# A graph kernel's hops: one tile of each group gathered by PE, three by Pool, where it was two and two or one and three

## The chip, the cores and the metric

The kernel runs on one core of one Trainium2 chip. The metric is the device time of one execution in microseconds; less is better.

The engines are PE (TensorE, matmuls; its weight loads are shown as PEld), DVE (VectorE), ACT (ScalarE), Pool (GpSimd) and SP (SyncE, which here only starts transfers). Each runs its own list of instructions in order and waits on semaphores that the others raise.

## The reference

A graph of 6250 nodes with 64 features and 200,000 edges, sorted by target node `dst` (in the reference's words the head), goes through two layers. The first is a relational attention of two hops, and it is the one that the change touches:

```python
def agg(emb):
    a_input = jnp.concatenate([emb[head], emb[tail]], axis=-1)
    h = a_input @ fc_w.T + fc_b
    e = jnp.sum(h * rel_e, axis=-1)            # rel_e = relation_emb[edge_type], 50 types
    e = jnp.where(e > 0, e, LEAKY_SLOPE * e)
    m = jax.ops.segment_max(e, head, num_segments=N)
    ex = jnp.exp(e - m[head])
    w = ex / jax.ops.segment_sum(ex, head, num_segments=N)[head]
    return jax.ops.segment_sum(emb[tail] * w[:, None], head, num_segments=N) + emb
...
for _ in range(2):
    emb = agg(emb)
    emb = emb / jnp.maximum(jnp.sqrt(jnp.sum(emb * emb, axis=-1, keepdims=True)), 1e-12)
```

Here `head` is `src` and `tail` is `dst`, by the order in which the edge index is stacked. Then come a residual and a layer norm, a graph convolution whose weights a GRU cell computes, and a second residual and norm.

## The kernel before

**First phase.** The edges are sorted into 50 blocks of 125 nodes by the node that receives. They are padded to tiles of 128 edges and groups of four tiles (512 edges), so that a group belongs to one block. Beside this PE streams the GRU weights. Within a block the edges are ordered by the other node, so the first tiles of a group, the low ones, often reach into only a few neighbouring blocks of the table of node rows. `tile_at` says which tile of each group is gathered near, and in which place; the lines around 766 build it.

**The two hops** (lines 1400 to 1675, the loop over `hop`) are the part that the change touches. In each hop, 408 groups go through a pipeline of nine stages. Step `i` works on group `i` in stage 0, on group `i-1` in stage 1, and so on; eight steps are written out and looped. All engines run the same order of steps:

- SP brings the words of a group four steps ahead: `lo_d` (which node of the block each edge has, broadcast) and `code_d` (the near nodes' code, broadcast), lines 1445 and 1446. After every four groups it brings the next row numbers, `stage_idx` (line 1439), once the four groups that used them have landed.
- Pool gathers the rows of the table for the tiles that PE does not take, one indirect DMA of 128 rows for a tile (line 1477). `rows` has room for eight groups, so Pool may start on a group when PE's sum of eight groups before is finished (`summed`). Where the next group's sum is already finished it goes on without a pause.
- DVE makes the near one-hot, `hot_near` (line 1660, stage 0), the one-hot of the node in the block, `hot_t` (line 1634), adds up `x_sum` (line 1618, stage 3: PE's product and the gathered row), picks the edge's type and makes the score, keeps the running maximum (line 1626) and adds the block's sum, `block_sum` (line 1668, stage 7).
- PE in one step, in this order: the weighted sum of stage 7 (`sums`, line 1543, raises `summed`), the score products of stage 2 (line 1533, `x_rdy`), the spread of stage 4 (line 1516), the turning of the probabilities of stage 6 (line 1524, `p_turned`), and the near gather of stage 1 (line 1507, `gathered`). The gather multiplies the one-hots in f32 with the blocks of the table in SBUF.
- ACT copies the turned probabilities to `prob` (line 1569; PE's next sum waits for it), takes the exponent, stores, copies the near rows to `rows` (line 1588) and computes the bound `lower` (line 1592), in this order.

How many tiles PE gathers follows from the group's place `u`:

```python
def near_tiles(u):
    return 2 - u % 2

def near_width(u):
    return (GW, GW + GW_B)[near_tiles(u) - 1]
```

So for even groups PE gathers two tiles, one over `GW` = 2 blocks and one over `GW_B` = 3, and Pool two; for odd groups PE gathers one over two blocks, and Pool three. Each block costs two f32 matmuls in the trace's count, so ten for an even group and four for an odd one. The input needs one sweep over the blocks.

**Last phase.** The graph convolution, with its own indirect gathers by Pool (line 1854), is not touched.

Of the kernel before, what the change touches and what calls it, by code (L numbers as in the profile page):

```python
# [5 lines left out]
ALU = mybir.AluOpType  # L6
# [118 lines left out]
def gnn_kernel(nc, x, src, dst, typ, relT, fc_w, fc_b, w_ih, w_hh, h_col, h_mat, b_ih, b_hh, out):  # L125
# [49 lines left out]
    GW, GW_B = 2, 3  # L175
# [16 lines left out]
    with ExitStack() as ctx:  # L192
# [51 lines left out]
        with ExitStack() as ph:  # L244
# [278 lines left out]
            def _(dve):  # L523
                link = Chain(dve, dv, dtick1)

                def block_of(to, nodes):
# [15 lines left out]
                                                   op0=ALU.mult, op1=ALU.add))  # L542
# [4 lines left out]
                                                   op0=ALU.mult, op1=ALU.add))  # L547
                link(dve.scalar_tensor_tensor(out=idx_i[:, 2, :], in0=idx_i[:, 0, :], scalar=6, in1=idx_i[:, 2, :],
                                              op0=ALU.logical_shift_left, op1=ALU.bitwise_or))
                dve.wait_ge(iota_rdy, 4)  # L550
                for to, t in ((sort_a, slice(0, BODY)), (sort_b, slice(BODY, ES))):
                    link.mark(dve.scalar_tensor_tensor(out=to[0:PS, t], in0=blk_i[:, t], scalar=13, in1=idx_i[:, 2, t],
                                                       op0=ALU.logical_shift_left, op1=ALU.bitwise_or))
# [15 lines left out]
                                                   op0=ALU.logical_shift_left, op1=ALU.bitwise_or))  # L569
# [47 lines left out]
                while m <= SORT:  # L617
                    if m > 512:
# [12 lines left out]
                                              op0=ALU.mult, op1=ALU.add))  # L631

                for to, v in ((run_n, counts), (run_left, left), (run_quads, quads), (run_base, base)):
# [9 lines left out]
                                              op0=ALU.mult, op1=ALU.add))  # L643
                link(dve.scalar_tensor_tensor(out=run_off[:, 0:DOWN], in0=run_off[:, 0:DOWN], scalar=-4.0, in1=run_n[:, 0:DOWN],
                                              op0=ALU.add, op1=ALU.add))
# [10 lines left out]
                                              op0=ALU.add, op1=ALU.mult))  # L656
                link(dve.tensor_scalar(no_quad, field, 0.0, None, ALU.is_equal))

                for c in range(len(CUTS) - 1):
# [3 lines left out]
                    for i, k in enumerate(run_order):  # L663
                        n = c * len(run_order) + i
                        dve.wait_ge(sign_rdy, n + 1)
                        if i == 0:
                            link(dve.scalar_tensor_tensor(out=to, in0=sign[:, n % 4, 0:w], scalar=4.0, in1=iota_f[:, t],
                                                          op0=ALU.mult, op1=ALU.mult))
                        dve.scalar_tensor_tensor(out=to, in0=sign[:, n % 4, 0:w], scalar=run_step[:, k:k + 1], in1=to,
                                                 op0=ALU.mult, op1=ALU.add).then_inc(sign_used, 1)  # L670
# [10 lines left out]
                for i in range(8):  # L681
                    v, q = i // 4, i % 4
# [9 lines left out]
                                              op0=ALU.is_lt, op1=ALU.mult))  # L692
# [11 lines left out]
                                              op0=ALU.mult, op1=ALU.add))  # L704
# [15 lines left out]
                for k in range(NB):  # L720
                    for w in range(3):
                        link.mark(dve.scalar_tensor_tensor(
                            out=picked_j, in0=iota_f[:, 0:QUADS], scalar=run_rest[:, k:k + 1],
                            in1=quad_words[:, :, w].bitcast(F32), op0=ALU.is_equal, op1=ALU.mult,
# [6 lines left out]
                                              in1=run_base[:, DOWN:NB], op0=ALU.mult, op1=ALU.add))  # L731
                link.mark(dve.scalar_tensor_tensor(out=one_at[:], in0=run_left[:], scalar=-1.0, in1=rest_at[:],
                                                   op0=ALU.add, op1=ALU.add))
# [27 lines left out]
                k_f, q_f, odd_f, is_a, is_b, is_r, low, tmp1 = (tile_c[:, j:j + 1] for j in range(8))  # L761
# [4 lines left out]
                link(dve.tensor_scalar(tile_k[:, 0:1], tile_k[:, 1:2], 1, None, ALU.bitwise_and))  # L766
                link(dve.tensor_copy(odd_f, tile_k[:, 0:1]))
                link.mark(dve.tensor_scalar(is_a, k_f, 0.0, None, ALU.is_equal))
                link.mark(dve.tensor_scalar(low, odd_f, -1.0, 1.0, ALU.mult, ALU.add))
                link.sync()  # L770
                link(dve.scalar_tensor_tensor(out=is_b, in0=k_f, scalar=1.0, in1=low, op0=ALU.is_equal, op1=ALU.mult))
                link(dve.tensor_tensor(is_r, is_a, is_b, ALU.add))
                link(dve.tensor_scalar(is_r, is_r, -1.0, 1.0, ALU.mult, ALU.add))
                link.mark(dve.tensor_tensor(low, is_b, is_r, ALU.subtract))
                link(dve.scalar_tensor_tensor(out=tmp1, in0=k_f, scalar=-2.0, in1=odd_f, op0=ALU.add, op1=ALU.add))
                link.mark(dve.tensor_tensor(tmp1, tmp1, is_r, ALU.mult))
                link(dve.scalar_tensor_tensor(out=k_f, in0=is_r, scalar=3.0, in1=is_a, op0=ALU.mult, op1=ALU.add))
                link(dve.tensor_scalar(is_a, is_a, -1.0, 1.0, ALU.mult, ALU.add))
                for j, v in enumerate((k_f, is_a, low, is_r, tmp1)):
                    link.mark(dve.tensor_copy(tile_w[:, j, 0:CHUNKS], v.broadcast_to([P, CHUNKS])))  # L780
                link.mark(dve.memset(tile_w[:, 0, CHUNKS:CHUNKS + 4], 1.0))
                link.mark(dve.memset(tile_w[:, 1:3, CHUNKS + 4:], 1.0))
# [25 lines left out]
                for v, j in ((tile_g[:, 0], 0), (tile_g[:, 2], 1), (tile_h[:, 0], 2), (tile_h[:, 2], 3)):  # L808
# [5 lines left out]
                                                   op0=ALU.mult, op1=ALU.add))  # L814
# [12 lines left out]
                                              op0=ALU.mult, op1=ALU.add))  # L827
                link(dve.tensor_tensor(tile_off[:], end_group[:], n_groups[:], ALU.subtract))
                link(dve.scalar_tensor_tensor(out=tile_off[:], in0=tile_off[:], scalar=float(KT), in1=n_tiles[:],
                                              op0=ALU.mult, op1=ALU.add))  # L830
# [10 lines left out]
                def listed(b0, n):  # L841
                    for b in range(n):
# [22 lines left out]
                                              scalar=-float(NODES), in1=dst_t[:], op0=ALU.mult, op1=ALU.add))  # L865
# [389 lines left out]
        for hop in range(2):  # L1255
            with ExitStack() as ph:
# [149 lines left out]

                def near_tiles(u):

                    return 2 - u % 2

                def near_width(u):

                    return (GW, GW + GW_B)[near_tiles(u) - 1]

                def per_land(u):

                    return (KT - near_tiles(u)) * 16
# [14 lines left out]
                with nc.Block() as block:  # L1432
                    @block.sync
                    def _(sp):
# [5 lines left out]
                        def head_rows(g, u):  # L1440
                            wait_tick(sp, tick, lo_in[u % 2], rows_in(g, u) - 32)
                            wait_tick(sp, tick, lower_rdy, g - 7)
                            wait_tick(sp, tick, hot_t_rdy, g - 7)
                            n = near_width(u) * P
                            sp.dma_start(lo_wide[:, u % 8], lo_d[ds(g, 1), :].broadcast_to([P, HEAD[0]])).then_inc(lo_in[u % 2], 16)
                            sp.dma_start(code_wide[:, u % 8, 0:n], code_d[ds(g, 1), 0:n].broadcast_to([P, n])
                                         ).then_inc(lo_in[u % 2], 16)
# [17 lines left out]
                    @block.gpsimd  # L1465
                    def _(pool):

                        def half(it, h):
                            g0 = it * 8 + h * 4
                            wait_tick(pool, tick, summed, g0 - 7)  # L1470
                            wait_tick(pool, tick, staged[h], it * 16 + 16)
                            for g in range(4):
                                if g:
                                    wait_tick(pool, tick, summed, g0 + g - 7)
                                for k in range(near_tiles(g), KT):
                                    j = g * KT + k
                                    pool.indirect_dma_start(  # L1477
                                        out=rows[:, h * 4 + g, k, :], out_offset=None, in_=tab_d[hop],
                                        in_offset=bass.IndirectOffsetOnAxis(ap=stage_idx[:, h, j:j + 1], axis=0)
                                    ).then_inc(landed[h * 4 + g], 16)  # L1480
                        pool_n = live(pool)
                        for h in range(2):
                            half(0, h)
                        with loop(pool, 1, pool_n) as it:
                            for h in range(2):
                                half(it, h)
# [111 lines left out]
                    def _(dve):  # L1598
# [4 lines left out]
                        link.mark(dve.memset(block_sum[:], 0.0))  # L1603

                        def body(i, u, stages, _):

                            if stages[5]:
# [46 lines left out]
                            if stages[0]:  # L1654
                                wait(dve, lo_in[u % 2], rows_in(i, u))
                                dve.sem_inc(dtick, 1)
                                with dve.bass.Fori(0, sweeps, 1, engines=(dve.engine,)) as t:
                                    dve.wait_ge(gathered, sweeps * i + (t + past))
                                    n = near_width(u)
                                    dve.tensor_scalar(hot_near[:, u % 2, 0:n].rearrange("p b e -> p (b e)"), code_wide[:, u % 8, 0:n * P],  # L1660
                                                      node_code[:, ds(t, 1)], None, ALU.is_equal).then_inc(near_rdy, 1)
# [16 lines left out]
        with ExitStack() as ph:  # L1678
# [134 lines left out]
            with nc.Block() as block:  # L1813
# [46 lines left out]
                def _(pe):  # L1860
# [8 lines left out]
                    def load(table, start, n, top):  # L1869
                        _, v = pe.bass.values_load_multi_w_load_instructions(  # L1870
                            table[0:1, ds(start, n)], engines=(pe.engine,), min_val=0, max_val=top,
                            skip_runtime_bounds_check_because="the table is held below the number of blocks")
                        return v
# [165 lines left out]
```

## Time and profile before

| | before |
|---|---|
| median of 3 runs | 7760.88 us (7728.9 to 7768.37) |
| profiled execution | 7748.06 us, its span 7746.2 us |
| mean granted PE clock | 0.739 |
| busy PE / DVE / Pool / ACT | 4691.7 / 4197.5 / 3271.4 / 2280.1 us |
| hop 1, hop 2 (first to last x_sum) | 1836.4 to 3925.2, 4050.5 to 6148.9 us |
| indirect gathers in the hops | 2040 |

The profile is that of one execution. A busy time is the sum over an engine's instructions. The idle time of a group of instructions is that of its engine just before them, with what ended it; "remote" is a release that the profile cannot put down to an instruction of this core, and "issue" is no wait that it shows. The ends of PE's instructions are modelled. PEclk is the granted clock of PE, 1.00 for 2.4 GHz and 0.50 for 1.2 GHz.

### The profile page before, as it was taken

How to read it: one execution, taken by the hardware profiler on the slowest of the kernel's cores; microseconds unless marked ns; L12 is line 12 of the kernel's file. 1: busy time of each engine (PE TensorE's matmuls, PEld its weight loads, DVE VectorE, ACT ScalarE, POOL GpSimd, SP SyncE). 2: the span in 40 equal slices, each digit the busy share in tenths (PEclk: the TensorE clock that was granted, in tenths of full speed). 3: DMA queues.
4: the chain of work that ended last, by engine and by line, in shares of the span. 5: the costliest groups of instructions: out<-in, count | busy, mean ns of one | idle time of the engine just before them, and what ended most of it. 6: DMA issues, size and time to landing. Idle time of an engine off the chain costs nothing. (4 is left out here: it accounts for less than half of the span.)

```text
span 7746.2 us, 194542 instructions
## 1 busy us (share of the span) xinstructions
PE 4691.7 (61%) x47798; PEld 3849.7 (50%) x47800; DVE 4197.5 (54%) x17518; ACT 2280.1 (29%) x5659; POOL 3271.4 (42%) x3384
## 2 busy tenths in 40 slices
PE   4210466614777777777747777777777646666664
PEld 0000011004666676766646667667666535555553
DVE  8300477945666666666656666666666633333334
ACT  4200000003444444444424444444444311111111
POOL 0677100143444444444424444444444335555553
PEclk7555688657888888888868788888888756666656
DMA  8311699913333333333323333333333212222211
GB/s 318 151 29 47 282 420 419 419 46 81 80 79 79 82 79 79 80 80 81 78 58 80 78 77 77 82 78 81 79 80 79 52 43 48 48 46 48 47 46 39
DMA packets 506838, 827.77 MB, mean 107 GB/s; under 512 B 159444, under 2 KB 411021, under 8 KB 457585
## 3 DMA queue, kind: packets, MB, share of 16 engines
q1 hardware_dynamic: 397729, 651.81, 26.5%
q0 software_dynamic: 107936, 174.35, 9.5%
q8 instruction: 57, 0.93, 0.0%
q10 hardware_dynamic: 1072, 0.31, 0.0%
q14 instruction: 44, 0.36, 0.0%
HBM read 810.55 MB, written 13.49 MB: 106 GB/s over the span
## 5 line engine op out<-in xcount | busy, mean ns | idle before, releaser
L1477 POOL DMA_INDIRECT rows<-tab_d,stage_idx x2040 | 1955.2, 958 | 2410.1 <-PE ps_g L1543 1501.9
L1543 PE MATMUL ps_g<-rows,arena 128*128 128x65 f32 x6528 | 1062.1, 316 | 1137.9 <-issue 797.2
L1543 PEld LDWEIGHTS ps_g<-rows,arena 128*128 128x128 f32 x6528 | 975.6, 229 | 1241.7 <-issue 1110.4
L1569 ACT ACTIVATE arena<-ps_p 128x512 f32<-128x512 f32 x816 | 487.2, 597 | 2290.4 <-remote 1137.4
L1854 POOL DMA_INDIRECT tab<-y_d,stage_src x768 | 725.8, 945 | 810.4 <-issue 279.2
L479 PE MATMUL ps_gate<-ring,h_sb 128*1 128x512 f32 x3072 | 564.3, 812 | 788.3 <-DMA ring<-w_ih 537.0
L1507 PE MATMUL ps_t<-tab,hot_near 128*128 x5712 | 921.7, 302 | 38.5 <-issue 34.9
L1507 PEld LDWEIGHTS ps_t<-tab,hot_near 128*128 128x128 f32 x5712 | 784.5, 208 | 63.0 <-issue 40.1
L1946 DVE TENSOR_SCALAR to_node<-wins_list,row_all 128x384 bf16<-128x384 bf16 x864 | 279.0, 336 | 918.7 <-remote 629.4
L1626 DVE CUSTOM_DVE_ANT_0 arena<-lower,ps_s,m_old 128x512 f32<-128x512 bf16 x816 | 610.3, 748 | 175.6 <-DVE x_sum L1618 112.7
L1645 DVE SCALAR_TENSOR_TENSOR picked<-iota_f,typ_e,x_sum 128x50 f32<-128x50 f32 x3264 | 686.2, 266 | 2.9 <-issue 2.8
L1660 DVE TENSOR_SCALAR hot_near<-arena,node_code 128x640 f32<-128x640 bf16 (+1 forms) x816 | 391.0, 479 | 506.1 <-issue 374.3
L1516 PE MATMUL ps_s<-ident_f,score 128*128 128x128 f32 x3264 | 614.2, 319 | 0.0
L1618 DVE TENSOR_TENSOR x_sum<-ps_x,rows 128x200 f32<-128x200 f32 x816 | 299.3, 367 | 578.8 <-remote 553.5
L420 POOL DMA_INDIRECT rec_d<-arena,row_all x438 | 445.7, 1018 | 360.6 <-DVEq L674 219.5
L1895 PE MATMUL ps_all<-arena,to_node 128*128 128x64 bf16 x7776 | 511.6, 232 | 132.5 <-issue 124.9
L1524 PE MATMUL ps_p<-ident_f,arena 128*128 128x128 f32 x3264 | 584.5, 310 | 4.2 <-issue 3.6
L479 PEld LDWEIGHTS ps_gate<-ring,h_sb 128*1 128x1 f32 x3072 | 41.8, 81 | 1097.0 <-DMA ring<-w_ih 690.0
L1592 ACT ACTIVATE lower<-arena,far_bias 128x512 bf16<-128x512 bf16 x816 | 583.4, 715 | 0.0
L1574 ACT ACTIVATE arena<-arena,m_new 128x512 f32<-128x512 f32 x816 | 581.5, 713 | 1.4 <-DVE m_diff L1639 0.7
L2008 ACT ACTIVATE arena<-ps_all 128x384 bf16<-128x384 f32 x432 | 211.7, 490 | 1244.9 <-PE ps_all L1882 684.7
L1895 PEld LDWEIGHTS ps_all<-arena,to_node 128*128 128x128 bf16 x7776 | 434.5, 119 | 212.0 <-issue 167.2
(455 smaller groups left out, 6730.5 us busy)
## 6 DMA issues: line engine op xcount, KB each, us to landing
ring<-w_ih SPq DMA_DIRECT2D x192, 1024.0 KB
ring<-w_hh SPq DMA_DIRECT2D x192, 1024.0 KB
arena<-lo_d SPq DMA_DIRECT2D x816, 128.0 KB
arena<-code_d SPq DMA_DIRECT2D x408, 160.0 KB
rows<-tab_d,stage_idx POOLq DMA_INDIRECT x2040
arena<-list_lo_d SPq DMA_DIRECT2D x216, 128.0 KB
arena<-code_d SPq DMA_DIRECT2D x408, 64.0 KB
tab<-y_d,stage_src POOLq DMA_INDIRECT x768
```

What stands on the lines that cost most here:

```text
L479: mm = pe.matmul(ps_gate[32 * j:32 * j + 1, r % 2, :], lhsT=h_sb[:, pc:pc + 1], rhs=ring[:, n % RING, j, :], start=(pc == 0), stop=(pc == ...
L1477: pool.indirect_dma_start(out=rows[:, h * 4 + g, k, :], out_offset=None, in_=tab_d[hop], in_offset=bass.IndirectOffsetOnAxis(ap=stage_idx[ ...
L1507: mm = pe.matmul(ps_t[:, k * TW:(k + 1) * TW], lhsT=hot_near[:, p, at0 + b, :], rhs=tab[:, ds(at + b, 1), 0:TW].rearrange("p a c -> p (a c)"),
L1516: mm = pe.transpose(ps_s[:, p, k * P:(k + 1) * P], score[:, p, k:k + 1].broadcast_to([P, P]), ident_f[:])
L1524: mm = pe.transpose(ps_p[:, k * P:(k + 1) * P], prob_t[:, p, k * P:(k + 1) * P], ident_f[:])
L1543: mm = pe.matmul(ps_g[:, p, 0:C + 1], lhsT=prob[:, p, k * P:(k + 1) * P], rhs=rows[:, u, k, 0:C + 1], start=(k == 0), stop=(k == KT - 1))
L1574: act.activation(prob_t[:, q, :], masked[:, q, :], ACT.Exp, bias=m_new[:, q:q + 1], scale=-1.0)
L1592: act.activation(lower[:, (u - 1) % 4, :], lo_wide[:, (u - 1) % 8, :], ACT.Abs, bias=far_bias[:], scale=BIG).then_inc(lower_rdy, 1)
L1626: link.mark(dve.tensor_tensor_reduce(masked[:, p, :], lower[:, (u - 5) % 4, :], ps_s[:, p, :], 1.0, m_old[:, p:p + 1], ALU.add, ALU.min, m ...
L1645: link.mark(dve.scalar_tensor_tensor(out=picked[:, k, :], in0=iota_f[:, 0:R], scalar=typ_e[:, ds(g * KT + k, 1)], in1=x_sum[:, k, :], op0= ...
L1854: pool.indirect_dma_start(out=rows[:, g, k].rearrange("p j c -> p (j c)"), out_offset=None, in_=y_d, in_offset=bass.IndirectOffsetOnAxis(a ...
L1895: mm = pe.matmul(ps_total[:, ds(slots[j % KT] + k, 1), :].rearrange("p a c -> p (a c)"), lhsT=to_node[:, j % 4, k * P:(k + 1) * P], rhs=go ...
```

## The change

Each group now has one tile gathered by PE, over two blocks, and three by Pool. `near_tiles` is 1 and `near_width` is `GW` for every `u`. With them the loops change: Pool's `for k in range(near_tiles(g), KT)` issues three gathers for each group, PE's `gather` has one part of two blocks (four matmuls), DVE's `hot_near` is 256 columns wide, ACT copies 115 columns, and SP brings 64 KB of code for each group. `per_land`, the count that readers of gathered rows wait for, is 48 for each group. The table `tile_at` is built so that the low tile stands in place 0 and the three others follow.

```diff
@@ -766,17 +766,17 @@
                 link.mark(dve.tensor_scalar(is_a, k_f, 0.0, None, ALU.is_equal))
-                link.mark(dve.tensor_scalar(low, odd_f, -1.0, 1.0, ALU.mult, ALU.add))
+                link.mark(dve.memset(low, 0.0))
...
-                link(dve.scalar_tensor_tensor(out=tmp1, in0=k_f, scalar=-2.0, in1=odd_f, op0=ALU.add, op1=ALU.add))
+                link(dve.tensor_scalar(tmp1, k_f, -1.0, None, ALU.add))
...
-                for j, v in enumerate((k_f, is_a, low, is_r, tmp1)):
+                for j, v in ((0, k_f), (1, is_a), (4, tmp1)):
                     link.mark(dve.tensor_copy(tile_w[:, j, 0:CHUNKS], v.broadcast_to([P, CHUNKS])))
@@ -1406,11 +1406,11 @@
 
                 def near_tiles(u):
 
-                    return 2 - u % 2
+                    return 1
 
                 def near_width(u):
 
-                    return (GW, GW + GW_B)[near_tiles(u) - 1]
+                    return GW
```

## Rows read from the trace of the kernel before

**Rows 1.** Groups of instructions by line and shape: count | busy us, mean ns | idle us before, releasers.

```profile
L1477 POOL DMA_INDIRECT rows<-tab_d,stage_idx x2040 | 1955.2, 958 | 2410.1 <-PE ps_g L1543 1501.9 <-issue 482.1 <-remote 278.3
...
L1507 PE MATMUL ps_t<-tab,hot_near 128*128 x5712 | 921.7, 302 | 38.5 <-issue 34.9 <-DVE hot_near L1660 0.9
...
L1660 DVE TENSOR_SCALAR hot_near<-arena,node_code 128x640 f32<-128x640 bf16 x408 | 245.4, 601 | 271.6 <-issue 186.6 <-DMA arena<-code_d 44.6 <-PE ps_t L1507 36.6
...
L1660 DVE TENSOR_SCALAR hot_near<-arena,node_code 128x256 f32<-128x256 bf16 x408 | 145.6, 357 | 234.4 <-issue 187.7 <-DMA arena<-code_d 39.9 <-remote 5.7
```

**Rows 2.** Line 1618 in hop 1, then hop 2: duration ns, first and last start us.

```profile
L1618 DVE TENSOR_TENSOR x_sum<-ps_x,rows x408: 358/367/368, 1836.4 to 3925.2; 128x200 f32<-128x200 f32 x136
...
L1618 DVE TENSOR_TENSOR x_sum<-ps_x,rows x408: 358/367/368, 4050.5 to 6148.9; 128x200 f32<-128x200 f32 x136
```

**Rows 3.** Table of waits over both hops: us in total, times, longest us.

```profile
ACT arena L1569 <- remote: 1137.4, 195, 8.1
...
DVE x_sum L1618 <- remote: 553.5, 173, 18.4
```

**Rows 4.** Timeline of Pool in one round of four: start us, us, operation, idle before.

```profile
3441.97 0.94 POOL L1477 DMA_INDIRECT rows<-tab_d,stage_idx  x1 [4.68 <-PE ps_g L1543]
3443.21 0.94 POOL L1477 DMA_INDIRECT rows<-tab_d,stage_idx  x1 [0.31 <-issue]
3446.11 1.16 POOL L1477 DMA_INDIRECT rows<-tab_d,stage_idx  x1 [1.96 <-PE ps_g L1543]
...
3448.83 0.97 POOL L1477 DMA_INDIRECT rows<-tab_d,stage_idx  x1 [0.30 <-issue]
3451.33 0.94 POOL L1477 DMA_INDIRECT rows<-tab_d,stage_idx  x1 [1.52 <-remote]
...
3453.84 0.94 POOL L1477 DMA_INDIRECT rows<-tab_d,stage_idx  x1 [0.30 <-issue]
...
3456.34 0.94 POOL L1477 DMA_INDIRECT rows<-tab_d,stage_idx  x1 [0.30 <-issue]
3462.39 0.94 POOL L1477 DMA_INDIRECT rows<-tab_d,stage_idx  x1 [5.12 <-PE ps_g L1543]
```

**Rows 5.** Timeline of PE in the same round, instructions of a kind merged.

```profile
3439.14 1.94 PE L1543 MATMUL ps_g<-rows,arena 128*128 128x65 f32 x8 [3.83 <-issue]
...
3443.13 1.35 PE L1507 MATMUL ps_t<-tab,hot_near 128*128 x10
3444.31 1.01 PE L1543 MATMUL ps_g<-rows,arena 128*128 128x65 f32 x8
...
3446.41 0.68 PE L1507 MATMUL ps_t<-tab,hot_near 128*128 x4
3447.27 1.08 PE L1543 MATMUL ps_g<-rows,arena 128*128 128x65 f32 x8 [0.19 <-issue]
...
3451.60 1.08 PE L1543 MATMUL ps_g<-rows,arena 128*128 128x65 f32 x8 [0.57 <-issue]
3452.51 0.47 PE L1533 MATMUL ps_x<-a_split,hot_t 128*128 x12
...
3459.50 1.94 PE L1543 MATMUL ps_g<-rows,arena 128*128 128x65 f32 x8 [5.07 <-issue]
```

**Rows 6.** Timelines of ACT, then DVE, in the same round.

```profile
3444.97 0.36 ACT L1588 ACTIVATE rows<-ps_t 128x230 f32<-128x230 f32 x1 [0.23 <-PE ps_t L1507]
...
3450.91 0.60 ACT L1569 ACTIVATE arena<-ps_p 128x512 f32<-128x512 f32 x1 [2.12 <-PE ps_p L1524]
...
3458.81 0.60 ACT L1569 ACTIVATE arena<-ps_p 128x512 f32<-128x512 f32 x1 [5.60 <-remote]
...
3450.80 0.28 DVE L1668 SCALAR_TENSOR_TENSOR block_sum<-block_sum,alpha,ps_g 128x65 f32<-128x65 f32 x1 [0.56 <-remote]
...
3458.79 0.37 DVE L1618 TENSOR_TENSOR x_sum<-ps_x,rows 128x200 f32<-128x200 f32 x1 [3.43 <-remote]
```

**Rows 7.** Busy time behind the long hold: PE, PEld, DVE, ACT, POOL, then PEclk.

```profile
3456.70:3463.50 6.80, 4.00 (x28) 3.97 (x29) 3.18 (x17) 2.21 (x6) 1.52 (x2) 0.50 0.22 64
```

## The prediction

> **What bounds the kernel now.** The page first. The change touches only the two hops, and the slices show them as two plateaus in which every engine is partly idle, the PE busiest at seven tenths. So no engine is the bound and the answer must lie in waits. The list of groups then gives the prices of the touched operations and the idle time of their engines [rows 1]: Pool is busy 1955.2 us with its 2040 indirect gathers and idle 2410.1 us before them. The first and last x_sum of each hop give its pace [rows 2]: (3925.2 - 1836.4) / 407 = 5.13 us a group in hop 1 and (6148.9 - 4050.5) / 407 = 5.16 us in hop 2, so 5.14 us for each of 816 groups.
>
> The table of waits shows where it goes [rows 3]. ACT's copy of prob waits 1137.4 us in 195 pieces, DVE's x_sum 553.5 us in 173 pieces, for something that the profile can only call remote. 173 pieces against 816 / 4 = 204 rounds of four groups: about once in four groups.
>
> So I took one such round apart. Pool's timeline [rows 4] shows not 2, 3, 2, 3 gathers with pauses, but runs of two (3441.97, 3443.21), three (3446.11 to 3448.83) and five (3451.33 to 3456.34, with 0.30 us between neighbours). PE's timeline [rows 5] shows its work of each step already finished when the readers start [rows 6]. The fourth step is the clear one: the score products L1533 end at 3452.51 + 0.47 = 3452.98, yet x_sum, which needs them and rows gathered a step or more earlier, starts at 3458.79; at 3458.81 ACT starts the prob copy, which needs other PE work of that step; and PE itself stands still for 5.07 us until 3459.50, because its next sum needs that copy. Two engines wake within 0.02 us, so it is not one late product: PE's completions as a whole became known together, 3458.79 - 3456.34 = 2.45 us after Pool's last issue of the run. The same after the run of three: PE's sum ends at 3447.27 + 1.08 = 3448.35, but block_sum, its reader, starts at 3450.80 and ACT at 3450.91, 1.97 and 2.08 us after the issue at 3448.83. After the run of two: gather ends at 3443.13 + 1.35 = 3444.48, ACT reads it at 3444.97, 1.76 us after 3443.21.
>
> What gets through tells when the hold begins. The sum that ends at 3451.60 + 1.08 = 3452.68, 1.35 us after the first issue of the run of five, was heard (Pool went on to the next group without a pause); L1533, 1.65 us after it, was not. My reading, an inference from these times: **while Pool issues indirect gathers back to back, completions of PE are not heard from 1.5 us after the first issue until about 2 us (three gathers) or 2.45 us (five) after the last.** That, not PE's work, paces the hops. The long hold also costs the clock: in the stretch behind it the granted clock is 0.50, 1.2 GHz [rows 7], and the eight matmuls of a sum take 1.94 us in place of 1.08 [rows 5].
>
> The Trainium skill (Perfetto Trace Analysis, Tensor Engine Instruction) says that the PE's end in a profile is computed, and that its semaphore update goes out once PSUM has acknowledged the writes. That leaves room for such a hold; no row here shows the acknowledgment.
>
> **The change part by part.** Before, of two groups PE gathers two tiles and one, Pool two and three. After, PE gathers one and Pool three in each.
>
> Removed from PE: of each pair of groups, six of 14 gather matmuls. The ten take 1.35 us and the four 0.68 [rows 5], so 0.67 us a pair, 408 x 0.67 = 273 us of PE work. DVE's hot_near goes from 601 to 357 ns [rows 1]: 0.24 us a pair, 100 us; it lies in the waits of rows 3 and I count it at nothing (at most 100 us if DVE were the bound). ACT's copy is half as wide and the code rows are 64 KB for each group; both lie beside waits, nothing. The table built in the first phase has two small copies and one operation less: nothing.
>
> Added: one gather more a pair, 408 in all, each 0.94 busy and 0.30 idle, 1.25 us from issue to issue [rows 4]: 510 us of Pool. Pool has 2410 us of idle, so as work it is covered. What it does to the holds is not. SP's staging of indices waits for three landings where it waited for two in every other group, and the head rows stand behind it on SP's queue; they are asked for four groups ahead, over 20 us, so nothing unless Pool falls a whole half behind.
>
> **The new round.** I follow the same rules from a long hold on; t = 0 is a sum heard while the clock is still low (3441.08). Now every group has three gathers.
>
> - Step A. Pool's first issue comes 0.9 us after the sum (3441.97 - 3441.08), the third at 0.9 + 2.5 = 3.4. PE would end its next sum at 3445.32 - 3441.08 - 0.67 = 3.6 us, but from 0.9 + 1.5 = 2.4 us on nothing is heard, until 3.4 + 1.95 = 5.35. Here the run of two let the sum through at 4.2. A costs 5.35; PE's saving vanishes in the hold.
> - Step B. The finished results come through at once. Before, the next sum ended 3452.68 - 3450.7 = 2.0 us after that, just before the next hold begins (Pool starts 0.65 us after, plus 1.5). If it does so again, B costs 2.1 us. But the gather's result is now held too, and with it ACT's copy of it and its lower bound, which stand ahead of the next prob copy on ACT; that can cost up to 0.5 us, and then B is held as A is: 5.2 us more, then 2.1.
> - Step C. Pool now has two groups back to back, six gathers where it had five: first issue 0.75 us after, last at 0.75 + 5 x 1.25 = 7.0. Released 2.6 later (1.76, 2.0, 2.45 us for two, three, five, so about 0.2 for each), at 9.6; the next sum is heard 3461.44 - 3458.79 = 2.65 us after release, low clock included: 12.25 us after B began. B and C together 12.25.
>
> Three steps: 5.35 + 12.25 = 17.6, 5.87 us a group. Four, with a second held step: 22.8, 5.70 us. I take 5.77, nearer to the four. Against 5.14 that is 0.63 x 816 = 514 us. The profiled execution took 7748.06 us (span 7746.2); 7748 + 514 = 8262. The median of three runs is 7760.88, 13 us above it, so I say 8270 us.
>
> **The rivals.**
> - *Mild.* Every sum falls just into the hold, so no two groups merge and no long run arises: each step 0.75 + 2.5 + 1.95 = 5.2 to 5.3 us. Then 0.06 to 0.16 x 816 = 50 to 130 us, 7810 to 7890 us. For it: only 0.15 us separates heard from held in step B. Against: 173 long waits in 204 rounds say that the sum usually gets through. Chance 0.15.
> - *Heavy.* A's sum slips through as well, so that only long rounds are left: 12.25 for two groups, 6.1 us, 8550 us and a little more. Needs a sum 1.2 us earlier than I find. Chance 0.07.
> - *Faster.* If the wait in rows 3 has nothing to do with Pool's runs, then PE's step counts, and its 0.67 us a pair come off: 7761 - 273 = 7490 us. It decides if x_sum's long wait ends at the same place with six gathers as with five. For it: PE is the busiest engine and Pool idles for 2410 us. Against: the two wakings 2.45 us after Pool's last issue. Chance 0.10.
> - *No effect.* Saving and loss cancel, or the gathers are hidden and PE's saving too: 7760. Chance 0.04.
>
> The third has a rule behind it: the Trainium skill (SBUF — State Buffer, Who interferes with whom) says that PE and ACT never wait on anyone and that DMA never contends with a compute engine. By that rule the added gathers cost nothing here and PE's saving stays. The trace of before does not agree: finished PE work is read up to 5.8 us late (3458.79 - 3452.98).
>
> **How the numbers follow.** The forecast has 0.64, with 8150 (5.6 us a group) to 8400 us (5.93) as its own range. To hold 8 in 10 the range reaches down into the mild case and a little above the forecast's: 7840 to 8470. Half a per cent, 39 us, is about what a measurement can tell from no change. Slower: 0.64 + 0.15 + 0.07 = 0.86. Within: 0.04. Faster: 0.10.
>
> **What would show each step.** Pool's timeline should have runs of three and of six, none of two or five, with the first reader of PE's work 2.6 us after the last issue of a six. L1477 should stand at x2448 and L1507 at x3264, PE's busy time lower though the hops are longer. x_sum's long waits should be about 4.5 us where they were 3.4, and come once in three or four groups. x_sum's first and last start should give 5.7 to 5.9 us a group. I am wrong if runs are only threes and steps 5.2 us (mild), if PE's results are read at once within a run (faster), or if x_sum waits for rows of its own group, which would be a landing and not a hold. The last phase, with its own gathers, should not move.

## The result and the profile after

The changed kernel takes 8257.02 us (median of 4 runs, 8253.36 to 8268.52) beside 7755.7 us for the kernel before (4 runs, 7728.9 to 7768.37): ratio 1.0654, 95% interval 1.0623 to 1.0685, so 6.5% slower. The forecast was 8270 us, slower. The profiled execution took 8253.68 us, span 8251.9. Of the executions behind the experiments below one was slow, at 11710.17 us with a granted clock of 0.411 (the kernel before, beside pool_alone_b and before_paced_b), and it stands in no ratio.

First the page's head and its 40 slices, with the count of instructions behind each engine's x.

```profile
span 8251.9 us, 187610 instructions
...
PE 4638.0 (56%) x45350; PEld 3783.4 (46%) x45352; DVE 4110.8 (50%) x17516; ACT 2222.2 (27%) x5659; POOL 3636.8 (44%) x3792
...
PE   4210566326666666666646666666666646666664
...
GB/s 324 127 27 47 385 419 420 244 50 68 67 69 69 68 69 67 66 68 69 68 55 66 69 69 68 68 68 69 70 66 68 68 31 48 48 47 47 47 48 39
```

The plateaus of the two hops are at six tenths of PE where they were at seven: more time, and fewer PE instructions in it (45350 where it was 47798).

Groups of instructions by line and shape, as [rows 1]:

```profile
L1477 POOL DMA_INDIRECT rows<-tab_d,stage_idx x2448 | 2319.5, 947 | 2559.7 <-PE ps_g L1543 1788.9 <-issue 587.2 <-DMA stage_idx<-dst_e 147.9
L1507 PE MATMUL ps_t<-tab,hot_near 128*128 x3264 | 654.5, 331 | 18.0 <-issue 17.3 <-DVE hot_near L1660 0.5
...
L1660 DVE TENSOR_SCALAR hot_near<-arena,node_code 128x256 f32<-128x256 bf16 x816 | 302.7, 371 | 488.9 <-issue 365.8 <-DMA arena<-code_d 96.5 <-remote 25.4
```

Pool has its 408 gathers more and is nevertheless idle longer before them, 2559.7 us where it was 2410.1. PE's gather matmuls fell by 921.7 - 654.5 = 267 us.

The first and last x_sum of each hop, as [rows 2]:

```profile
L1618 DVE TENSOR_TENSOR x_sum<-ps_x,rows x408: 361/367/369, 1817.1 to 4184.6; 128x200 f32<-128x200 f32 x136
...
L1618 DVE TENSOR_TENSOR x_sum<-ps_x,rows x408: 353/367/369, 4299.9 to 6655.3; 128x200 f32<-128x200 f32 x136
```

(4184.6 - 1817.1) / 407 = 5.82 us a group in hop 1 and (6655.3 - 4299.9) / 407 = 5.79 us in hop 2, where [rows 2] gave 5.13 and 5.16. That is 0.66 x 816 = 537 us in the hops. Some 29 us come back ahead of hop 1 (x_sum starts at 1817.1, not 1836.4) and between the hops (115.3 us, not 125.3). The stretch from the last x_sum to the end is 8251.9 - 6655.3 = 1596.6 us, before 1597.3.

The table of waits over both hops, as [rows 3] (us in total, times, longest):

```profile
ACT arena L1569 <- remote: 1740.3, 251, 7.6
...
DVE x_sum L1618 <- remote: 1131.0, 243, 13.9
```

x_sum waits 1131.0 / 243 = 4.65 us each time (before 553.5 / 173 = 3.2), once in 816 / 243 = 3.4 groups.

One round of the changed kernel. Pool's timeline, as [rows 4]:

```profile
3490.48 0.94 POOL L1477 DMA_INDIRECT rows<-tab_d,stage_idx  x1 [5.31 <-PE ps_g L1543]
...
3492.97 0.96 POOL L1477 DMA_INDIRECT rows<-tab_d,stage_idx  x1 [0.30 <-issue]
3495.69 0.94 POOL L1477 DMA_INDIRECT rows<-tab_d,stage_idx  x1 [1.76 <-PE ps_g L1543]
...
3502.03 0.95 POOL L1477 DMA_INDIRECT rows<-tab_d,stage_idx  x1 [0.30 <-issue]
3507.93 0.95 POOL L1477 DMA_INDIRECT rows<-tab_d,stage_idx  x1 [4.95 <-PE ps_g L1543]
```

PE's, as [rows 5]:

```profile
3492.68 1.08 PE L1543 MATMUL ps_g<-rows,arena 128*128 128x65 f32 x8 [0.19 <-issue]
...
3495.90 1.08 PE L1543 MATMUL ps_g<-rows,arena 128*128 128x65 f32 x8 [0.39 <-issue]
3496.82 0.47 PE L1533 MATMUL ps_x<-a_split,hot_t 128*128 x12
...
3505.20 1.94 PE L1543 MATMUL ps_g<-rows,arena 128*128 128x65 f32 x8 [6.46 <-issue]
```

ACT's and DVE's, as [rows 6]:

```profile
3504.50 0.60 ACT L1569 ACTIVATE arena<-ps_p 128x512 f32<-128x512 f32 x1 [7.09 <-remote]
...
3495.17 0.28 DVE L1668 SCALAR_TENSOR_TENSOR block_sum<-block_sum,alpha,ps_g 128x65 f32<-128x65 f32 x1 [0.69 <-PE ps_g L1543]
...
3504.49 0.37 DVE L1618 TENSOR_TENSOR x_sum<-ps_x,rows 128x200 f32<-128x200 f32 x1 [4.89 <-remote]
```

The reader is to see a run of three (3490.48 to 3492.97), then six (3495.69 to 3502.03). The sum that ends at 3492.68 + 1.08 = 3493.76 is read by block_sum only at 3495.17, 2.20 us after the last issue of the three. The score products end at 3496.82 + 0.47 = 3497.29 and x_sum starts at 3504.49, 7.2 us later and 2.46 us after the last issue of the six; ACT starts 0.01 us after it. The window behind it, as [rows 7]:

```profile
3504.40:3508.50 4.10, 3.30 (x25) 3.33 (x26) 3.00 (x17) 2.21 (x6) 0.57 (x1) 0.50 0.23 65
```

The granted clock is again 0.50 (1.2 GHz), and the sum takes 1.94 us in place of 1.08.

### The profile page after: what moved, and what is told of

Same layout as the page of the kernel before. It is cut to its first block and busy times, and to the rows that moved or that the text cites. A ratio compares the mean times of both kernels' runs of the same rounds, so it can differ in the third digit from the quotient of the medians.

```text
span 8251.9 us, 187610 instructions
## 1 busy us (share of the span) xinstructions
PE 4638.0 (56%) x45350; PEld 3783.4 (46%) x45352; DVE 4110.8 (50%) x17516; ACT 2222.2 (27%) x5659; POOL 3636.8 (44%) x3792
## 5 line engine op out<-in xcount | busy, mean ns | idle before, releaser
L1477 POOL DMA_INDIRECT rows<-tab_d,stage_idx x2448 | 2319.5, 947 | 2559.7 <-PE ps_g L1543 1788.9
L1543 PE MATMUL ps_g<-rows,arena 128*128 128x65 f32 x6528 | 1154.2, 334 | 1718.3 <-issue 1253.9
L1543 PEld LDWEIGHTS ps_g<-rows,arena 128*128 128x128 f32 x6528 | 1059.3, 246 | 1824.2 <-issue 1556.1
L1569 ACT ACTIVATE arena<-ps_p 128x512 f32<-128x512 f32 x816 | 487.2, 597 | 2892.9 <-remote 1740.3
L479 PE MATMUL ps_gate<-ring,h_sb 128*1 128x512 f32 x3072 | 573.1, 824 | 776.7 <-DMA ring<-w_ih 548.3
L1618 DVE TENSOR_TENSOR x_sum<-ps_x,rows 128x200 f32<-128x200 f32 x816 | 299.4, 367 | 1144.7 <-remote 1131.0
L1626 DVE CUSTOM_DVE_ANT_0 arena<-lower,ps_s,m_old 128x512 f32<-128x512 bf16 x816 | 610.2, 748 | 200.8 <-DVE x_sum L1618 111.6
L1516 PE MATMUL ps_s<-ident_f,score 128*128 128x128 f32 x3264 | 664.6, 339 | 0.1
L1507 PE MATMUL ps_t<-tab,hot_near 128*128 x3264 | 654.5, 331 | 18.0 <-issue 17.3
L1524 PE MATMUL ps_p<-ident_f,arena 128*128 128x128 f32 x3264 | 630.9, 329 | 0.8 <-ACT alpha L1576 0.7
L420 POOL DMA_INDIRECT rec_d<-arena,row_all x438 | 445.9, 1018 | 360.2 <-DVEq L674 219.5
L1574 ACT ACTIVATE arena<-arena,m_new 128x512 f32<-128x512 f32 x816 | 581.2, 712 | 0.4 <-DVE m_diff L1639 0.4
L1660 DVE TENSOR_SCALAR hot_near<-arena,node_code 128x256 f32<-128x256 bf16 x816 | 302.7, 371 | 488.9 <-issue 365.8
L1507 PEld LDWEIGHTS ps_t<-tab,hot_near 128*128 128x128 f32 x3264 | 524.8, 229 | 42.1 <-issue 18.8
L479 PEld LDWEIGHTS ps_gate<-ring,h_sb 128*1 128x1 f32 x3072 | 41.9, 81 | 1093.7 <-DMA ring<-w_ih 705.5
```

The lines of the kernel that those rows point to most:

```text
L479: mm = pe.matmul(ps_gate[32 * j:32 * j + 1, r % 2, :], lhsT=h_sb[:, pc:pc + 1], rhs=ring[:, n % RING, j, :], start=(pc == 0), stop=(pc == ...
L1477: pool.indirect_dma_start(out=rows[:, h * 4 + g, k, :], out_offset=None, in_=tab_d[hop], in_offset=bass.IndirectOffsetOnAxis(ap=stage_idx[ ...
L1507: mm = pe.matmul(ps_t[:, k * TW:(k + 1) * TW], lhsT=hot_near[:, p, at0 + b, :], rhs=tab[:, ds(at + b, 1), 0:TW].rearrange("p a c -> p (a c)"),
L1516: mm = pe.transpose(ps_s[:, p, k * P:(k + 1) * P], score[:, p, k:k + 1].broadcast_to([P, P]), ident_f[:])
L1524: mm = pe.transpose(ps_p[:, k * P:(k + 1) * P], prob_t[:, p, k * P:(k + 1) * P], ident_f[:])
L1543: mm = pe.matmul(ps_g[:, p, 0:C + 1], lhsT=prob[:, p, k * P:(k + 1) * P], rhs=rows[:, u, k, 0:C + 1], start=(k == 0), stop=(k == KT - 1))
```

## The experiments

The first eight kernels, and two of the last four, met chips on which the kernel before takes 5936 to 5942 us, not 7756. Those six chips turned out to be a control of their own; the last two kernels met a chip on which it takes 7744. No chip was met twice in the experiments, so whether the difference lies in the chip or in a state it was in is not known; "chip" below means the chip as it was met.

**Theory.** The hold that the prediction read from the trace: the length of Pool's runs of indirect gathers decides how long PE's results are not heard. **Rivals.** The gathers' own work or landing makes the loss, or PE's, ACT's and DVE's parts of the change do.

**pe_alone.** PE leaves six matmuls of each pair out, and DVE, ACT and SP do only what they do in the changed kernel; Pool stays as before. So nobody gathers the second tile of even groups: its rows stay zero, and the kernel does not compute the reference's values.

```
+def pool_from(u):
+    return 2 - u % 2
-for k in range(near_tiles(g), KT):
+for k in range(pool_from(g), KT):
```

> PE's part of the change alone: one near tile for each group on PE, DVE, ACT and SP as in the changed kernel, but Pool's gathers stay 2, 3, 2, 3; the second tile of even groups is left out (its rows are zero). Theory of the hold: Pool's runs stay two, three and five, the long hold stays, and only the step behind it, the one whose sum gets through, is shorter by up to 0.67 us in a round of four: 204 x 0.67 = 137 us, so about 7620 us. Rival (PE's work paces the hops): 273 us less, 7490 us. Rival (nothing of PE counts): 7760 us.

5890.95 us beside 5941.27: ratio 0.9914 (0.9897 to 0.993).

**pool_alone.** The opposite: PE's fourteen matmuls stay, and in even groups Pool gathers a third tile too, into a buffer that nobody reads. Whoever reads the group's rows waits for its landing too (`per_land` is 48).

```
+if near_tiles(g) == 2:
+    pool.indirect_dma_start(out=unused[:, h * 2 + g // 2, :], ...)
```

> Pool's part alone: the kernel before with its PE work, but in even groups Pool issues one gather more, into a spare tile that nobody reads, and readers of the rows wait for its landing too. Theory of the hold: runs of three and six, 5.8 us a group or a little more, 8250 to 8350 us. Rival (Pool's added issues are covered by its idle time): 7760 us. Rival (the loss comes from reading rows that PE no longer supplies): 7760 us too.

5911.79 us beside 5941.27: ratio 0.995 (0.9933 to 0.9966). The added gathers cost nothing on this chip; the kernel is even 0.5% faster.

**after_paced and before_paced.** One wait more on Pool ahead of each group's gathers, in the kernel after and in the one before: it takes them up only when PE has also turned the probabilities of the step whose sum it waits for (`p_turned`). No work is added or left out; the wait is meant to keep the gathers of two groups apart.

```
 wait_tick(pool, tick, summed, g0 - 7)
+wait_tick(pool, tick, p_turned, g0 - 6)
...
 wait_tick(pool, tick, summed, g0 + g - 7)
+wait_tick(pool, tick, p_turned, g0 + g - 6)
```

> The changed kernel with one wait more on Pool: before a group's gathers it also waits until PE has turned the probabilities of the same step. Theory of the hold: that completion is held during a run, so two groups can't merge, all runs are of three, and each step costs about 0.75 + 2.5 + 1.95 = 5.2 us: 816 x 0.6 less, about 7780 us. Rival (Pool is too slow with three gathers, or rows land too late): an added wait can only make it later, 8260 us or more.

> The kernel before with the same added wait on Pool. Theory of the hold: runs of two and three in turn, none of five; a step with a run of three costs 5.2 us, one with a run of two is let through at about 4.2 us, 4.7 us on average where it was 5.14: 0.44 x 816 = 360 us less, about 7400 us. Rival: 7760 us or more.

5889.64 us (0.991, 0.9893 to 0.9926) and 5913.86 us (0.9952, 0.9936 to 0.9969). No theory had expected any of these four times, since all counted from 7756 or 8257. Nor does the pause do here what it was meant to: the trace of before_paced still has 87 runs of five gathers in hop 1, so on this chip it says nothing on the length of the runs. Something else was different, and the next runs asked what.

**probe_hold.** A kernel by itself, with none of the case's computation: PE and ACT hand a one-column product to and fro 760 times, DVE copies one column in a chain, and Pool meanwhile issues runs of 1 to 8 indirect gathers.

```
for j in range(n):
    pool.indirect_dma_start(out=got[:, j, :], in_=pairs, in_offset=idx[:, j:j + 1], ...)
...
pe.wait_ge(taken, t); pe.matmul(ps[:, 0:1], ...).then_inc(made, 1)
act.wait_ge(made, t + 1); act.activation(took[:], ps[:, 0:1], ACT.Copy).then_inc(taken, 1)
```

> This kernel computes nothing of the reference: it copies x to the output, and beside that PE and ACT play ping-pong (one small matmul, one small copy of it, each waiting for the other), DVE runs a chain of small copies that wait for each other, and Pool issues runs of 1, 2, 3, 4, 5, 6 and 8 indirect gathers of 128 rows of 512 bytes, then runs of 3 and 6 plain transfers; then SP issues 3 and 6. Theory of the hold: in each run of n indirect gathers ACT does not hear PE from about 1.5 us after the first issue until about 2 us after the last, so the gap between two ACT copies is about 1.25 (n - 1) + 0.5 us or more, 1.8 us for two, 3.0 for three, 5.5 for five, 6.8 for six, while DVE's chain goes on without a gap. SP's transfers leave no gap. For Pool's plain transfers it says nothing. Rival (the readers in the hops wait for their own rows to land, or for Pool): no gap in any run, since nothing here waits for a landing but Pool.

The table of waits of probe_hold:

```profile
PEld ps L66 <- ACT took L72: 261.0, 759, 0.3
...
PE ps L66 <- ACT took L72: 199.5, 759, 0.3
```

Of 759 waits of PE for ACT none is over 0.3 us, with up to eight gathers back to back; each turn takes 0.446 to 0.448 us. There is no hold here. The kernel before took 5939.43 us beside it.

**after_again and before_again.** The two kernels unaltered.

> The changed kernel itself, unaltered, beside the kernel before on whichever chip this job gets. In the jobs so far the kernel before took 5941 and 5939 us, 1815 us less than in the runs shown with the result, and the ping-pong of PE and ACT went on every 0.446 us through all of Pool's gathers: no hold there. Theory of the hold: the loss of 6.5% is made by the hold alone. Where the kernel before takes about 5940 us, the changed one then gains what it takes off PE and DVE, 0 to 1.5%, 5850 to 5940 us; where it takes about 7756 us, the changed one is again at 8257 us. Rival (Pool's third gather costs by its own time or its landing): 3 to 6% slower on either chip.

> The kernel before, unaltered, as one of the runs, so that its trace can be read on a chip of this job. Theory of the hold: if it takes about 5940 us, its trace shows x_sum and ACT's prob copy without the 2 to 6 us waits behind Pool's runs, the hops at about 4.2 us a group, and in the first phase the weights streaming on through Pool's long run of scatters, where the trace shown with the prediction has 29 and 47 GB/s in two slices. Rival (chips of these jobs are quicker all over): instructions and landings themselves are shorter in the same proportion, 23%. The ratio to the kernel before, which is itself, shows what a comparison of this kind can tell.

5881.71 us beside 5940.91: ratio 0.9902 (0.9886 to 0.9919); and 5942.05 us, ratio to itself 1.0002. **The same change is 1.0% faster here and 6.5% slower there.** The chips hardly differ in how fast Pool, DVE and ACT execute: L1477 has a mean of 955 ns in before_again (958 there), DVE's L1626 748 (748), ACT's L1569 597 (597). PE's matmuls are shorter (L1543 277 ns, 316 there) at a higher granted clock (0.889, there 0.739), but PE's busy time differs by only 4691.7 - 4378.6 = 313 us of the 1810 between the spans. The rest lies in waits. Page slices, then the table of waits from 1180 to 4420 us (hop 1 and most of hop 2), of before_again:

```profile
GB/s 288 413 419 418 417 418 397 16 109 99 99 99 99 98 97 96 99 99 99 65 88 98 97 96 97 99 96 95 98 98 95 97 20 68 69 69 69 68 70 49
...
ACT arena L1569 <- PE ps_p L1524: 945.4, 726, 2.9
POOL rows L1477 <- PE ps_g L1543: 807.4, 412, 4.3
...
ACT arena L1574 <- DVE m_diff L1639: 377.8, 646, 2.8
```

ACT's copy has no wait for something remote, where [rows 3] has 195; nor has it any when the table is taken over both hops. Pool's timeline of before_again, then ACT's and DVE's beside it, with a run of five:

```profile
2023.35 0.94 POOL L1477 DMA_INDIRECT rows<-tab_d,stage_idx  x1 [3.34 <-PE ps_g L1543]
...
2028.35 0.94 POOL L1477 DMA_INDIRECT rows<-tab_d,stage_idx  x1 [0.30 <-issue]
```

```profile
2028.00 0.60 ACT L1569 ACTIVATE arena<-ps_p 128x512 f32<-128x512 f32 x1 [1.11 <-PE ps_p L1524]
...
2027.50 0.37 DVE L1618 TENSOR_TENSOR x_sum<-ps_x,rows 128x200 f32<-128x200 f32 x1
```

x_sum and ACT's copy start 4.15 and 4.65 us into the run, before its last issue; where the hold is, both came 2.45 us after it [rows 4, 6].

**wide_near.** The changed kernel with near_width left at (GW + GW_B, GW) in turn, so that DVE's and SP's part isn't narrower. This asks where the 1% comes from. ACT's copy stays half as wide, as in the changed kernel.

> The changed kernel with one part undone: in even groups SP brings 160 KB of code and DVE makes hot_near 640 columns wide again, of which PE reads only the first 256. PE, ACT and Pool stay as changed. On a chip without the hold DVE starts x_sum without waiting, so the theory there is that DVE's own time paces the hops, and that the 1% that the changed kernel gains is the narrower hot_near: 563 - 358 = 205 ns x 408 = 84 us at most, 59 measured. Then this kernel is back at the time of the kernel before, 5930 to 5945 us. Rival (PE's six matmuls for each pair make the gain): it stays at about 5882 us. If the job gets a chip where the kernel before takes about 7756 us, DVE's width lies in the holds and this kernel takes 8257 us as the changed one.

5892.5 us beside 5940.52: 0.9921 (0.9908 to 0.9935). My theory that DVE's width makes the gain fell: most of it stays. pe_alone at 0.9914 has PE's shorter step and ACT's narrower copy in common with it, and these are the likely source; no run takes the two apart. Since pool_alone and before_paced, in which PE saves nothing, also gain 0.5%, a part of the 1% may have another source. The 11 us between wide_near and after_again lie between different chips, and I don't read them.

**probe_b and after_paced_b.** A further try at meeting the other kind of chip.

> The same probe as before, on whatever machine it meets. If the kernel before takes about 5940 us beside it, both theories expect the ping-pong of PE and ACT at 0.45 us throughout. If the kernel before takes about 7756 us beside it, the theory of a hold by Pool's gathers expects the ping-pong to stop 1 to 2 us after the first of a run of gathers and to resume 1.8 to 2.6 us after the last, gaps of some 4 us for a run of three and 8 us for one of six to eight; the rival, that the machine is slow for another reason, expects 0.45 us there too.

> The changed kernel whose Pool waits for the last turned product before each run of a group. If the kernel before takes about 5940 us beside it, 5890 us, as this kernel did before. If the kernel before takes about 7756 us beside it: by the theory of the hold Pool's runs stay short, one group each, so that PE is heard once in every group and the kernel takes about 7780 us, against 8257 for the changed kernel unpaced; by the rival, that the gathers' own work or landing costs the time, a pause can only add, 8260 us or more.

Not met: the kernel before took 5936.2 us, the probe 366.07 with the same waits, after_paced_b 5889.65 (0.9918, 0.9902 to 0.9935).

**pool_alone_b and before_paced_b.** The same two kernels as above, on a chip where the kernel before takes 7743.66 us.

> The kernel before with Pool's third gather in every group and PE's six matmuls kept. If the kernel before takes about 5940 us beside it, 5912 us, as this kernel did before. If it takes about 7756 us beside it: by the theory of the hold, runs of three and six set the pace whatever PE does, and it takes 8250 to 8350 us, as the whole change; by the rival, that the loss comes from PE's or ACT's part, about 7760.

> The kernel before with Pool's pause ahead of each run. If the unpaced one takes about 5940 us beside it, 5914 us, as this kernel did before. If it takes about 7756 us beside it: by the theory of the hold no run of five arises any more, each group is released about 2 us after its two or three gathers, and it takes about 7400 us; by the rival, that a run's length doesn't matter, a pause can only add, 7760 or more.

pool_alone_b: 8274.52 us, ratio 1.0685 (1.066 to 1.0711). before_paced_b: 7427.11 us, ratio 0.959 (0.9567 to 0.9613). Both fall where the theory of the hold had them, 8250 to 8350 and 7400, and neither is where a rival had it. x_sum's first and last start in hop 1, pool_alone_b, then before_paced_b:

```profile
L1624 DVE TENSOR_TENSOR x_sum<-ps_x,rows x408: 351/367/368, 1837.8 to 4189.6; 128x200 f32<-128x200 f32 x136
```

```profile
L1620 DVE TENSOR_TENSOR x_sum<-ps_x,rows x408: 358/367/369, 1832.4 to 3773.0; 128x200 f32<-128x200 f32 x136
```

5.78 us a group with Pool's part alone (the whole change 5.82), and (3773.0 - 1832.4) / 407 = 4.77 us with the pause (unpaced 5.13). Pool's timeline of before_paced_b, then ACT's:

```profile
3001.35 0.94 POOL L1479 DMA_INDIRECT rows<-tab_d,stage_idx  x1 [1.82 <-PE ps_p L1526]
...
3003.87 0.95 POOL L1479 DMA_INDIRECT rows<-tab_d,stage_idx  x1 [0.30 <-issue]
3006.73 0.94 POOL L1479 DMA_INDIRECT rows<-tab_d,stage_idx  x1 [1.91 <-remote]
3007.98 0.94 POOL L1479 DMA_INDIRECT rows<-tab_d,stage_idx  x1 [0.31 <-issue]
3010.62 0.94 POOL L1479 DMA_INDIRECT rows<-tab_d,stage_idx  x1 [1.70 <-PE ps_p L1526]
```

```profile
3005.98 0.60 ACT L1571 ACTIVATE arena<-ps_p 128x512 f32<-128x512 f32 x1 [3.10 <-remote]
...
3009.87 0.60 ACT L1571 ACTIVATE arena<-ps_p 128x512 f32<-128x512 f32 x1 [1.58 <-PE ps_p L1526]
```

A run of three, a run of two, and the next begins: in this stretch the run of five is gone (8 are left in hop 1, table below), and each run is released 2.11 us (3005.98 - 3003.87) or 1.89 us (3009.87 - 3007.98) after its last issue. Counted from Pool's and ACT's timelines over hop 1 (a run is gathers under 1.5 us from start to start; the release is ACT's next prob copy after its last issue):

| kernel | kernel before takes, us | runs of 2 / 3 / 5 / 6 | release after 3, median us | after 5 or 6 |
|---|---|---|---|---|
| before | 7756 | 106 / 103 / 89 / 0 | 2.25 | 2.48 |
| after | 7756 | 10 / 150 / 0 / 116 | 2.27 | 2.56 |
| pool_alone_b | 7744 | 7 / 173 / 4 / 105 | 2.76 | 2.70 |
| before_paced_b | 7744 | 190 / 191 / 8 / 0 | 2.10 | 2.61 |
| before_again | 5942 | 47 / 61 / 119 / 0 | 2.90 | 0.26 |

In before_again runs of five are even more frequent, 119, and ACT's copy comes 0.26 us after their last issue. There the time after a run is set by the work, not by the run.

One more count over hop 1 turns the reading of one round into one of all. Take, for each run of five or six gathers, the stretch from 2 us after its first issue to 1.5 us after its last. In before no prob copy of ACT starts in any of the 89 stretches, in after in none of 116, in pool_alone_b in none of 109; in before_again one starts in each of the 119. In the program this copy waits for `p_turned` and `summed` alone, which PE raises; a row that lands late can't hold it, unless PE's own work is late by it, and in the rounds shown PE's products stand as ended.

## Why the prediction was right

**The reading of the waits holds.** The hold was an inference from one round; two things carry it now. On a chip that has it, adding gathers alone, with PE's, ACT's and DVE's work unchanged, makes the whole loss (1.0685; the change itself 1.0654, the intervals overlap). And spreading the same 2040 gathers, with no work changed, wins 4.1%. On two of the six other chips, where the traces show no hold, the added gathers cost nothing (pool_alone 0.995, the whole change 0.9902). What is shown is that the length of Pool's runs sets the pace there, on the one chip where both kernels were run. That it is PE's completions that go unheard rests on the timelines alone: they can't tell it from readers that wake late, nor, since PE's ends are modelled, from products that really end late.

**PE's saving vanishes in the hold: right.** Priced at 273 us, measured 267 us of the gather matmuls; pool_alone_b, which keeps them, is no slower by the intervals. PE's total fell only from 4691.7 to 4638.0 us, since the granted clock fell too (mean 0.739 to 0.709) and the other matmuls grew longer (L1543 from 316 to 334 ns).

**DVE, ACT and SP at nothing: right** within what the runs tell, for the same reason: pool_alone_b leaves their work as it was and is slower by as much.

**Step A**, 5.35 us, and **steps B and C**, 12.25 us: in the round shown the heard sums end at 3489.70, 3493.76 (read at 3495.17), 3496.98 and 3507.14. From 3489.70 to the reading at 3495.17 are 5.47 us, and from there to 3507.14 are 11.97: three steps in 17.44 us, 5.81 each, against 17.6 forecast. The release, 2.6 us after the last issue of a six, measured 2.46 here and 2.56 in the median. The mean of both hops is 5.80 us a group where I took 5.77, so the round of three steps is nearer than the one of four that I leaned to. The hops took 537 us where I said 514; the 29 us given back outside them were in no term, and the two misses nearly cancel, which is luck.

Three small slips were without effect: x_sum's waits before were 553.5 / 173 = 3.2 us each, not 3.4; DVE has two instructions less in the first phase (17518 to 17516), not three; and ten runs of two are left in hop 1, where there should be none.

**The rivals.** *Mild* fell: 116 runs of six in hop 1. *Heavy* fell: 150 runs of three are left. *No effect* fell. *Faster* (7490) fell on this chip, but its mechanism, PE's shorter step counts, is the likely reading of the chips without the hold: ratios 0.9914 without Pool's part of the change and 0.9902 with the whole. The change is worth 59 us there and not 273. I take it that only a part of PE's step is on the path, as ACT's L1574 waits 377.8 us for DVE's m_diff in before_again; no run shows it. The Trainium skill (SBUF — State Buffer, Who interferes with whom) says that PE and ACT never wait on anyone and that DMA never contends with a compute engine. The page says this of the ports of SBUF. The prediction's step from there, that added gathers cost nothing, agrees with pool_alone on a chip without the hold (0.995); where the kernel before takes 7744 us, adding gathers alone gives a ratio of 1.0685, and there the measurement decides against that step. It doesn't show a conflict of ports, so the rule itself is neither confirmed nor refuted.

**What stays open.** Why one chip has the hold and another not, and whether it keeps it. Whether the probe would show it directly, and what after_paced takes there (about 7780 by the theory): neither met such a chip. Why pool_alone and before_paced gain 0.5% on a chip without the hold.

## What to carry to other kernels

Where two engines on different work wake within 0.02 us of each other, look for what a third had just stopped doing, and count its runs, not its busy time: 510 us of "covered" gathers cost 537 us in the hops. An idle engine that runs ahead can be worth a pause: one wait that keeps nearly all of Pool's runs to a single group won 4.1% where the hold is, and the same wait lost nothing (0.5% faster) where it isn't. And time a change on more than one chip before its sign is believed, with the kernel before beside it each time.

## What the runs showed of the hardware

Not expected at all: the same program takes 7744 to 7756 us on some chips and 5936 to 5942 us on six others, with Pool's, DVE's and ACT's instructions of the hops nearly equal in length, and one change is 6.5% slower on the one kind and 1.0% faster on the other.

The loss isn't a matter of the hops alone. In the first phase Pool issues 438 indirect scatters (L420), from 232 to 818 us in before. Two slices inside that stretch (387 to 775 us) have only 29 and 47 GB/s in before, and the same two have 30 and 41 in before_paced_b; before_again keeps 413 to 419 GB/s from 148 to 890 us, while its scatters run from 232 to 924. PE's last matmul on the streamed weights (L479) starts at 1570.5 us in before and at 1032.8 in before_again. The kernel before reaches its first x_sum at 1836.4 us there and at 1235.2 us in before_again (601 us less), needs 5.14 and 4.21 us a group in the hops (760 us), and 1597.3 and 5935.6 - 4775.9 = 1159.7 us after the last x_sum (438 us), where Pool gathers once more: together 1799 of the 1810 us between the two. These three stretches are nearly the whole kernel, so the split says only that each of them, and each has indirect transfers by Pool, is slower. That scatters or gathers cause it outside the hops is not shown: no run changed them.

The page rows of the scatters, before_again:

```profile
L420 POOL DMA_INDIRECT rec_d<-arena,row_all x438 | 547.1, 1249 | 365.1 <-DVEq L674 219.6
```

and before_paced_b:

```profile
L420 POOL DMA_INDIRECT rec_d<-arena,row_all x438 | 449.4, 1026 | 357.2 <-DVEq L674 219.9
```

The mean scatter is 0.22 us shorter where the kernel is slower. That is not each of them: the medians are 966 and 958 ns, and 182 of the 438 take over 1.2 us in before_again, 16 in before_paced_b.
